# Windowed attention: the negated, scaled row maxima go from VectorE to GpSimd, and their sign is taken in VectorE's maximum

## What is computed

```python
for i in range(DEPTH):                       # 6 layers, 16 heads of 64, windows of 32
    x = attn_layer(shift_tokens(x), ...) + x
    x = ffn_layer(shift_tokens(x), ...) + x

# inside attn_layer: q, k have unit length per head, then a rotary table is applied
sim = jnp.einsum('bhwie,bhwje->bhwij', bq, bk2) * QK_SCALE   # 32 queries, 64 keys
sim = jnp.where(mask, -jnp.finfo(sim.dtype).max, sim)
attn = jax.nn.softmax(sim, -1)
out = jnp.einsum('bhwij,bhwje->bhwie', attn, bv2)
```

## Time and profile before

| what | us |
|---|---|
| three runs | 5861.93, 5877.77, 5872.63 |
| median | 5872.63 |
| profiled execution, its own time | 5863.98 |
| profiled execution, span of the trace | 5862.2 |
| the windowed layers within the span | 2222 to 5790 |

### The profile page before, as it was taken

How to read it: one execution, slowest core, us unless ns; L and a number is a source line. 1 busy time by engine, 2 the same in 40 slices (tenths; PEclk the granted TensorE clock), 3 DMA queues, 4 the chain that set the end, 5 groups by cost and what they waited for, 6 DMA issues and landing times. The chain is left out here.

```text
span 5862.2 us, 231052 instructions
## 1 busy us (share of the span) xinstructions
PE 4926.6 (84%) x94976; PEld 3059.6 (52%) x95234; DVE 4495.5 (77%) x9185; ACT 3552.5 (61%) x9917; POOL 2732.6 (47%) x2368
## 2 busy tenths in 40 slices
PE   5888888765777757899999999999999999999996
PEld 2222222222333325666666666666666666666663
DVE  5777777566655656788888888888888888888884
ACT  1455555432444435677777777777777777777774
POOL 0000000001000016777777777777777777777772
PEclk9999999887999978999999999999999999999997
DMA  4001010012111110111111111011111111111010
GB/s 120 12 12 17 12 17 12 34 55 57 18 20 23 19 46 24 30 29 36 38 30 28 35 37 32 27 36 38 30 29 36 38 30 29 36 38 28 28 28 29
DMA packets 89273, 186.23 MB, mean 32 GB/s; under 512 B 19159, under 2 KB 45719, under 8 KB 88471
## 3 DMA queue, kind: packets, MB, share of 16 engines
q1 hardware_dynamic: 84188, 182.96, 11.8%
q10 hardware_dynamic: 4896, 0.84, 0.1%
HBM read 54.15 MB, written 27.26 MB: 14 GB/s over the span
## 5 line engine op out<-in xcount | busy, mean ns | idle before, releaser
L371 DVE TENSOR_REDUCE a_mpart<-a_pr 128x1 f32<-128x512 f32 (+2 forms) x1904 | 1105.3, 629 | 482.0 <-PE a_pr L456 274.2
L612 ACT ACTIVATE a_probs<-a_ps 128x1024 f32<-128x1024 f32 (+3 forms) x896 | 802.1, 932 | 910.6 <-PE a_ps L474 440.8
L1563 ACT ACTIVATE w_probs<-w_pa,w_nm,w_rqs 128x64 f32<-128x64 f32 x3072 | 1218.3, 449 | 0.0
L1563 ACT ACTIVATION_READ_ACCUMULATOR w_probs<-w_pa,w_nm,w_rqs 128x1 f32 x3072 | 768.9, 250 | 0.0
L474 PE MATMUL a_ps<-a_QS,a_KS 128*128 128x512 bf16 (+3 forms) x1719 | 501.2, 374 | 277.1 <-ACT a_probs L612 153.5
L1556 ACT ACTIVATE w_sq<-w_pr 128x512 f32<-128x512 f32 x768 | 457.5, 609 | 431.5 <-DVE w_sinb L1702 430.4
L456 PE MATMUL a_pr<-a_KS,a_QS 128*128 128x512 bf16 (+3 forms) x1815 | 608.3, 380 | 92.3 <-DMA a_QS<-a_norows 78.4
L338 POOL COPY a_V<-a_vals 128x288 f32 (+1 forms) x32 | 14.3, 455 | 1437.8 <-PE a_po L492 1437.7
L1268 POOL TENSOR_TENSOR w_sinb<-w_sinb,w_tabk 128x512 f32<-128x512 f32 x384 | 489.0, 1274 | 355.2 <-DVE w_sinb L1702 355.2
L1268 POOL TENSOR_TENSOR w_sinb<-w_sinb,w_tabq 128x512 f32<-128x512 f32 x384 | 524.1, 1365 | 152.7 <-DVE w_sinb L1702 152.7
L1702 DVE STREAM_SHUFFLE w_sinb<-w_pr 128x512 f32<-128x512 f32 x768 | 564.2, 735 | 0.0
(11 more groups left out here) (223 smaller groups left out, 9888.7 us busy)
## 6 DMA issues: line engine op xcount, KB each, us to landing
w_Vp<-w_V SPq DMA_DIRECT2D x192, 384.0 KB, 3.5
w_Vp<-w_V SPq DMA_DIRECT2D x192, 128.0 KB, 3.4
a_QS<-q_parts SPq DMA_DIRECT2D x34, 384.0 KB
a_KS<-k_parts SPq DMA_DIRECT2D x34, 384.0 KB
q_parts<-a1p_part SPq DMA_DIRECT2D x48, 128.0 KB, 1.8
k_parts<-a1p_part SPq DMA_DIRECT2D x48, 128.0 KB, 1.8
q_parts<-a2p_part SPq DMA_DIRECT2D x48, 128.0 KB, 1.8
k_parts<-a2p_part SPq DMA_DIRECT2D x48, 128.0 KB, 1.8
```

Of the source, the lines that this page charges most:

```text
L371: nc.vector.reduce_max(mpart[:, h, qt, kc:kc + 1], p_r[:, at["chunk", k] % 3, 0:width], AX_X).then_inc(max_read, 1)
L612: nc.scalar.activation(probs[:, s % 2, 2 * pair:2 * pair + 2, c0:CH], p_s[:, pair, :, c0:CH], ACT.Exp, scale=SM_SCALE).then_inc(exped, 1)
L1563: op = nc.scalar.activation(probs[:, g, t, c, :], s_of(g)[:, t, c, :], ACT.Exp, bias=nm[:, g, t, c:c + 1], scale=scale_of(g)[:, t, c:c + 1 ...
```

## The change

The maximum is now a `tensor_reduce` with `negate=True`, so that `mx` holds the negated maximum. The product with `scale_of(g)` is a `tensor_tensor` on GpSimd, in the new function `shift(g, m)`, one for each of the four groups. VectorE no longer waits for its own maximum and has one instruction fewer per group. It waits instead for GpSimd's reading of the previous pair's `mx`.

```diff
--- before.py
+++ after.py
@@ -1288,6 +1288,12 @@
                         notfirst[:, ds(m % PPB, 1)].unsqueeze(2).broadcast_to([P, 8, WIN]),
                         ALU.mult).then_inc(S["kcarry"], 1)
 
+                def shift(g, m):
+                    pool.wait_ge(S[f"mx{g}"], m + 1 + FIRST)
+                    pool.wait_ge(S[f"ex{g}"], m + FIRST)
+                    nc.gpsimd.tensor_tensor(nm[:, g, :, :], mx[:, g, :].rearrange("p (t c) -> p t c", t=2),
+                                            scale_of(g), ALU.mult).then_inc(S[f"nm{g}"], 1)
+
                 def scale_probs(g, m):
                     pool.wait_ge(S[f"rden{g}"], m + 1 + FIRST)
                     p = probs[:, g, :, :, :].rearrange("p t c j -> p (t c) j")
@@ -1295,12 +1301,19 @@
                                             ALU.mult).then_inc(S[f"pn{g}"], 1)
 
                 def turn(n):
+                    if on(n, 2):
+                        shift(0, n - 2)
                     if on(n, 0):
                         table_k(n)
+                    if on(n, 2):
+                        shift(1, n - 2)
                     if on(n, 1):
                         rotate(6, n - 1)
                         rotate(7, n - 1)
                         carry_k(n - 1)
+                    if on(n, 2):
+                        shift(2, n - 2)
+                    if on(n, 1):
                         rotate(5, n - 1)
                     if on(n, 2):
                         scale_probs(3, n - 2)
@@ -1319,6 +1332,8 @@
                         rotate(3, n)
                         rotate(2, n)
                         rotate(0, n)
+                    if on(n, 1):
+                        shift(3, n - 1)
 
                 pool.wait_ge(S["xs"], 4 + FIRST)
                 for n in range(3):
@@ -1707,12 +1722,9 @@
                     if g == 3:
                         dve.wait_ge(S["scored"], m + 1 + FIRST)
                         dve.wait_ge(S["rqs"], m + 1 + FIRST)
-                    nc.vector.reduce_max(mx[:, g, :], s_of(g).rearrange("p t c j -> p (t c) j"),
-                                         AX_X).then_inc(S[f"mx{g}"], 1)
-                    dve.wait_ge(S[f"mx{g}"], m + 1 + FIRST)
-                    nc.vector.scalar_tensor_tensor(
-                        nm[:, g, :, :].rearrange("p t c -> p (t c)"), mx[:, g, :], -1.0,
-                        scale_of(g).rearrange("p t c -> p (t c)"), ALU.mult, ALU.mult).then_inc(S[f"nm{g}"], 1)
+                    dve.wait_ge(S[f"nm{g}"], m + FIRST)
+                    nc.vector.tensor_reduce(mx[:, g, :], s_of(g).rearrange("p t c j -> p (t c) j"),
+                                            AX_X, ALU.max, negate=True).then_inc(S[f"mx{g}"], 1)
 
                 def denominator(g, m):
                     dve.wait_ge(S[f"ex{g}"], m + 1 + FIRST)
```

## The result

The changed kernel takes 5809.39 us (median of four executions, 5797.19 to 5812.03), against 5875.2 for the kernel before (four executions too). The ratio is 0.9887, with a 95% interval of 0.9864 to 0.9909, so it is faster by 1.1%. I had forecast 5822 within 5730 to 5905, with faster at 0.62.

What follows compares the result with a forecast made beforehand. VectorE's chain to `three`, with ScalarE's close second, and TensorE's low clock bound the turn; 35.50 + 0.66 us plus a little low clock gives 36.2 against 36.74, 48 us over 88 turns: 5822 us, range 5730 to 5905.

Steps and rivals of the forecast that it cites:

- What VectorE loses: VectorE without its four products: `products(6)` 0.39 us earlier, `residual` at 9 to 10, removing TensorE's 2.01 us wait.
- What a GpSimd product costs: Each small product moved to GpSimd was taken at 0.15 us, with 0.40 as the upper estimate.
- GpSimd's list and who waits for it: `rotate(6)` waits for `maximum(1)`, starting 1.69 us later; VectorE's `turn_probs(1)` starts at 16.65, 0.4 late.
- The port waits behind it: VectorE's Newton products wait for GpSimd's `table_q` and `scale_probs(0)`, 0.26 us more; `three` done at 23.5.
- The clock: TensorE's low clock behind its wait ahead of `centre`, 1.68 us per long turn, was expected nearly gone.
- undisturbed turn: A windowed-layer turn without the low clock: 35.50 us before, forecast at 36.16 after the change.
- turns still come in two lengths: Sign of a wrong prediction in the windowed layers; it expected turns of one length, near 36.2 us.
- The first six turns: The few turns at the start, left out of the sum over 88 turns, as were those at the end.
- A: Rival: VectorE gets away from GpSimd, turns end with ScalarE's chain at 35.0 us, about 5715; chance 0.17.
- ScalarE's chain: Work from `keep_v(0)` to `square(3)`, meeting VectorE's chain at TensorE; put some 0.6 us shorter, the close second bound.
- C: Rival: the late `three` ahead of `turn_back` causes the low clock; slower, 5917 or 5975, above 5890; chance 0.22.
- B: Rival: gain cancels through a costlier GpSimd product or another port wait; turns 36.6 to 36.8, within 0.3%; chance 0.16.

Runs made afterwards that it cites:

- e2: The change with the product of group 1 written behind `rotate(6)` in GpSimd's list instead of ahead of it; 5745.44 us, 0.9777 of the kernel before.
- e3: The change with `maximum(2)` and three extra VectorE reductions ahead of `residual`, to make it late again; 5875.24 us, 0.9993 of the kernel before.
- e7: The change with group 1's product behind `rotate(6)` and group 2's behind `rotate(5)` on GpSimd; 5652.33 us, 0.9621 of the kernel before.
- e9: e7 with the GpSimd products of groups 3 and 0 made twice, first into an extra tile; 5648.92 us, 0.962 of the kernel before.
- e5: The change with only the products of groups 3 and 0 on GpSimd, the others on VectorE; 5721.03 us, 0.9739 of the kernel before.
- e4: The change with each of GpSimd's four products made twice, first into an extra tile; 5896.55 us, 1.003 of the kernel before.
- e6: The change with only the products of groups 1 and 2 on GpSimd, the others on VectorE; 5875.36 us, 1.0005 of the kernel before.
- e1: The kernel before with the sign taken in the maximum, the product still on VectorE as a `tensor_tensor`; 5876.9 us, 1.0004 of the kernel before.

## Why the prediction was right

*What VectorE loses.* Right. `products(6)` came at 1.99 (forecast 1.95), `maximum(1)` ended at 5.12 (5.08), and `residual` was done at 9.26 (9 to 10). One wait was not in my sum: L1772, the layer norm's scaling, grew from a mean of 416 to 990 ns, since it now meets a running GpSimd instruction: in the turn above it ends at 3571.42, 0.15 us behind the GpSimd product that ends at 3571.27. A little earlier L1763, which took 1487 ns before, takes 427. Together they are 0.5 us shorter, which is in the 9.26.

*What a GpSimd product costs.* Mis-sized: 0.21 us where I took 0.15, with 0.17 us from one start to the next where two run back to back. The product of group 1, the one ahead of `rotate(6)`, takes 0.32 in the rows above. The Trainium skill, *GPSIMD Engine Reference*, § 4.1 Engine selection, has GpSimd at about twice VectorE's time with two inputs. The rows do not agree for this shape: 211 ns against 0.17 us, a factor of 1.2. Against VectorE's mean with its waits, 694 ns, GpSimd is the faster place.

*GpSimd's list and who waits for it.* Right: `rotate(6)` at 5.48 (forecast 5.45), `turn_probs(1)` at 16.34 (16.65). Undoing just this delay (e2) gave 0.51 us per turn. I had 0.3 us too much in it, and this is most of why the turn is 35.79 and not 36.16.

*The port waits behind it.* `three` was done at 23.14 (23.5), 6.80 us behind the start of `turn_probs(1)`, against 6.59 before. I had 0.26 for this; it is 0.21.

*The clock.* Right in its sign, and it is the whole gain. By the lengths of the turns, the average was 36.74 - 35.50 = 1.24 us above an undisturbed turn and is now 36.10 - 35.79 = 0.31 above it. That is 0.93 won, of which the undisturbed turn gives back 0.29. e3 takes the clock's part away and leaves nothing. I had forecast nearly no low clock (0.04 us a turn), and this term was too small: twelve turns of 37.0 to 37.1 remain, and five more at layer boundaries, which were long before as well. So turns still come in two lengths, which the prediction had named as a sign of being wrong. The granted clock between 3400 and 4600 is 0.99. A fall costs 1.2 to 1.3 us in the changed kernel, not 1.68. This error and the undisturbed turn's went opposite ways, so the mean of 36.10 against a forecast of 36.2 is closer than its parts, by luck.

*The first six turns.* Left out of the sum as few, and they lost 11.1 us. That the 88 turns gave 8.3 us more than forecast covered most of it, by luck again. In the other kernels the six turns take 251.7 to 260.1 us, against 248.8 before. The granted clock in them is 0.91 before and in e2 (251.9 us), 0.89 after, and 0.87 in e7 (259.6). After the change TensorE's busy time in them is 6.6 us above that of before. That fits a clock falling more often between the longer waits there, but no experiment tried it. e9, whose common turn is that of e7, takes 254.3 us for them, so a part of it may change from one execution to the next. The cause stays open.

*The rivals.* A's turn of 35.0 was to be had without GpSimd's delay (35.28 in e2, 35.05 in e5, 34.28 in e7), though by another order of the list, not by chance. It is no floor, since e7 lies below it, and in none of the three does ScalarE's chain set the turn by these rows: TensorE waits for `three` behind `square(3)` in e2 and e5, and in e7 ScalarE has about 0.2 us to spare (e9). C was nearer than its text says: 0.3 us more wait for `three` and it is there (e4, e6). Its argument that a unit between the two idle pieces protects the clock did not hold, since e4's long turns have 0.60 and 1.49 us of idle time around that unit. B was not seen in the change. e6 has B's time, since a gain and a loss of one size cancel there, but by C's mechanism: turns of two lengths, 46 of them long with the low clock.

## What to carry to other kernels

When a small operation goes to an engine that works strictly through a list, what counts is not its own 0.2 us but what it holds up while it waits for its input. Write it behind work that doesn't need that input: the same four products gave 1.1%, 2.2% and 3.8% in three places. And look behind TensorE's longest idle time for the granted clock, even where that wait is hidden: here the 1.7 us that most turns paid were gone in the kernel with 0.3 us less of that wait (e5), and 0.3 us more of another (e4) made most turns long again.

## What I had not expected of the hardware

- An idle time ahead of `centre` of 2.0 to 2.1 us was followed by the low clock, a granted clock of 0.5, in some two of three turns (before, e1, e3), one of 1.71 (e5) or 0.92 (e7) in none of the common turns. Two pieces of 0.60 and 1.20 us with a unit of 1.13 between them, counted by its row, came with it in 12 of 88 turns (the change), of 0.60 and mostly 1.5 in 60 of 88 (e4), and of 0.60 and 1.4 to 1.6 in 46 of 88 (e6). So the length of the waits alone does not tell which turns fall.
- VectorE's `TENSOR_SCALAR` from SBUF to SBUF, 128 x 256 in f32, has one tensor operand and still waits like the instructions with two operands in SBUF. It takes 0.41 us in the kernel before, where the GpSimd instruction that runs at its start ends 0.2 us later, and 0.99 in the change, where that one ends 0.8 us later.
- A product of 128 x 8 on GpSimd takes 0.21 us, a fifth of the 1.04 for 128 x 512, with 64 times fewer elements.
